# V products and their copies moved to other slots of the batch loop, in a gated cross-attention and expert block

## The reference

```python
# attention over the context, 16 heads of depth 8
q = layernorm(x) @ Wq.T + bq ; k = ctx @ Wk.T + bk ; v = ctx @ Wv.T + bv
attn = softmax(q k^T / sqrt(8))                    # per batch and head: 56 x 1500
x = x + tanh(g_xattn) * ((attn @ v) @ Wo.T + bo)
# 160 experts, the 8 with the highest sigmoid router score, and a shared expert
x = x + tanh(g_ffn) * ffn(layernorm(x))
```

## Time and profile before

| | |
|---|---|
| median of 3 runs | 1201.7 us (1195.89 to 1203.61) |
| the profiled execution | 1199.14 us, of which its span is 1197.6 us |
| granted TensorE clock, mean | 0.979 of full speed |
| instructions | 37,798 |

### The profile page before, as it was taken

One profiled execution on the slowest core, in us unless ns is written; L12 is line 12 of the kernel. 1 busy time (PEld: TensorE's weight loads), 2 busy tenths in 40 slices (PEclk: granted clock), 3 DMA queues, 4 the chain that ended last, 5 costly groups with the idle time before them and its releaser, 6 DMA issues.

```text
span 1197.6 us, 37798 instructions
## 1 busy us (share of the span) xinstructions
PE 1099.4 (92%) x12090; PEld 704.8 (59%) x12090; DVE 979.5 (82%) x1680; ACT 837.8 (70%) x1790; POOL 599.5 (50%) x1011
## 2 busy tenths in 40 slices
PE   1586989999999999999999999877999999999998
PEld 0254667767766667767766676653555555555554
DVE  2774768878788788787887888757999999999998
ACT  1343656676666676676667666656888888888887
POOL 7887588888888887888888772000000000000000
PEclk9887999999999999999999999988999999999999
DMA  8869668969878789798887863123777676777773
GB/s 134 156 124 162 140 134 174 151 149 166 145 163 154 139 169 146 152 164 145 168 151 139 168 118 74 41 90 108 225 234 234 223 240 222 236 230 229 237 224 125
DMA packets 200998, 197.04 MB, mean 165 GB/s; under 512 B 161183, under 2 KB 167391, under 8 KB 200966
## 3 DMA queue, kind: packets, MB, share of 16 engines
q1 hardware_dynamic: 189446, 175.64, 65.4%
q0 software_dynamic: 11520, 20.99, 7.0%
HBM read 109.96 MB, written 12.55 MB: 102 GB/s over the span
## 4 chain that ended last, share of the span: by engine, by line
PE 75%; DVE 7%; ACT 5%; issue 4%; DMA 4%; SPq 3%; POOL 2%; ACTq 0%; DVEq 0%; POOLq 0%
PE bank L1230 14%; PE bank L1258 14%; PE bank L1069 12%; PE bank L1083 12%; PE bank L1100 8%; PE bank L1136 5%; ACT p_exp L640 4%; PE bank L1124 4%; DMA ctT<-ctx_parts 3%; DVE rec L938 2%; DVE part_max L838 1%; SPq L378 1%; PE bank L1155 1%; DVE ctT L980 1%; PE bank L1148 1%
## 5 line engine op out<-in xcount | busy, mean ns | idle before, releaser
L640 ACT ACTIVATE p_exp<-bank 125x448 f32<-125x448 f32 x768 | 389.6, 546 | 241.9 <-PE bank L1083 241.3
L838 DVE TENSOR_REDUCE part_max<-bank 128x1 f32<-128x500 f32 x672 | 419.5, 671 | 111.5 <-PE bank L1100 110.9
L1083 PE MATMUL bank<-q_st,k_stk 97*125 97x224 f16 x1536 | 282.9, 268 | 23.7 <-ACT p_exp L640 6.9
L1100 PE MATMUL bank<-kparts,q_blk 128*128 128x500 f16 x672 | 256.3, 384 | 17.8 <-DVE part_max L838 13.2
L1083 PEld LDWEIGHTS bank<-q_st,k_stk 97*125 97x125 f16 x1536 | 184.2, 138 | 130.4 <-ACT p_exp L640 75.9
L1258 PE MATMUL bank<-ctT,w_ring 128*128 128x448 f16 x960 | 234.0, 353 | 3.0 <-DVE ctT L980 3.0
L732 ACT ACTIVATE ctT<-bank 128x448 f32<-128x448 f32 x320 | 174.0, 544 | 40.0 <-PE bank L1230 15.8
L980 DVE TENSOR_TENSOR ctT<-k_stk,ctT 128x448 f16<-128x448 f32 x320 | 198.0, 619 | 0.3 <-ACT ctT L738 0.2
L1069 PE MATMUL bank<-p_exp,v_sb 125*25 125x168 f32 (+1 forms) x6144 | 189.2, 264 | 0.6 <-ACT p_exp L640 0.6
L738 ACT ACTIVATE ctT<-k_stk 128x448 f16<-128x448 f32 x320 | 181.9, 568 | 3.5 <-DVE k_stk L974 3.5
L1230 PE MATMUL bank<-q_hi,w_ring 128*128 128x448 f16 x640 | 173.9, 353 | 2.2 <-ACT k_stk L720 2.2
(11 more groups left out here) (139 smaller groups left out, 1244.8 us busy)
## 6 DMA issues: line engine op xcount, KB each, us to landing
v_sb<-c_scratch SPq DMA_DIRECT2D x114, 448.0 KB, 3.9
k_stk<-kparts SPq DMA_DIRECT2D x384, 93.8 KB, 5.0
ctx_in<-in_ctx_dram SPq DMA_DIRECT2D x31, 750.0 KB
k_stk<-c_scratch SPq DMA_DIRECT2D x38, 448.0 KB, 4.0
w_scratch<-w_out POOLq DMA_DIRECT2D x80, 128.0 KB, 6.7
w_in<-in_L_ffn_w_gate_dram POOLq DMA_DIRECT2D x160, 32.0 KB, 4.5
w_in<-in_L_ffn_w_down_dram POOLq DMA_DIRECT2D x80, 64.0 KB, 7.7
v_sb<-c_scratch SPq DMA_DIRECT2D x6, 336.0 KB, 4.8
```

Source lines behind the costliest of these rows:

```text
L640: act.activation(p_exp[0:KP, j % PR, f * 448:(f + 1) * 448], ST[f][0:KP, 0:448], ACT.Exp).then_inc(exp_done, 1)
L838: v.reduce_max(part_max[:, i // NCH, i % NCH:i % NCH + 1], SM[i % NSM][:, 0:CK], axis=AX.X).then_inc(sm_maxed, 1)
L1083: last = pe.matmul(ST[f][0:KP, (g % 2) * GC:(g % 2 + 1) * GC], k_stk[0:97, u, g, j * KP:(j + 1) * KP], q_st[0:97, u, g, :, :].rearrange("p ...
L1100: pe.matmul(SM[i % NSM][:, 0:CK], rows, kparts[:, u, 0, c * CK:(c + 1) * CK], start=True, stop=True).then_inc(sm_done, 1)
```

## The change

The V products of a chunk move from slots 3, 7, 11 to slots 0, 4, 8. ScalarE's copies of V move from behind the second exponential of slots 4, 8 and 0 of the next step to behind the first exponential of slots 1, 5, 9; the copies now wait chunk by chunk for the value products that read the old contents. The spread product and the normalisation move from slot 5 to slot 6, the product with Wo from slot 9 to slot 11, behind the transpose of the maxima, and the update of x to the end of slot 11. The waits that guard bank 6 move with them. No instruction that computes or copies is added or removed.

```diff
-    SPREAD_AT, OUT_AT, NEG_AT = 5, 9, KT - 1
+    SPREAD_AT, OUT_AT, NEG_AT = 6, KT - 1, KT - 1
...
                         if f == 0:
                             evacuate(step, k - 1)
-                    if k == 0 and on(step, 2):
-                        values(back(step, 2), NCH - 1)
-                    elif k and k % TPC == 0 and on(step, 1):
-                        values(back(step, 1), (k - 1) // TPC)
+                        if f == 0 and k % TPC == 1 and on(step, 1):
+                            values(back(step, 1), k // TPC)
...
                 act.wait_ge(vp_done, b * NCH + (c + 1))
-                if c == 0:
-                    until(act, pv_done, (b - 1) * KT)
+                until(act, pv_done, (b - 2) * KT + (c + 1) * TPC)
...
+                evacuate(step, KT - 1)
...
-                    if on(step, 1) and k % TPC == 3:
+                    if on(step, 1) and k % TPC == 0:
                         u = back(step, 1)[1]
                         b = num(back(step, 1))
                         until(pe, v_copied, b * NCH + c)
-                        if on(step, 3) and c == 1:
+                        if on(step, 4) and c == 0 and back(step, 4)[1] == 1:
+                            pe.wait_ge(x2_done, back(step, 4)[0] + 1)
+                        if on(step, 3) and c == 2:
                             pe.wait_ge(nrm_done, num(back(step, 3)) + 1)
-                        if on(step, 3) and c == 2 and back(step, 3)[1] == 1:
-                            pe.wait_ge(x2_done, back(step, 3)[0] + 1)
...
-                            pe.wait_ge(v_copied, num(back(step, 1)) * NCH + 1)
+                            pe.wait_ge(v_copied, num(back(step, 1)) * NCH + 2)
...
+                    if on(step, 1) and k == NEG_AT:
+                        b = num(back(step, 1))
+                        pe.wait_ge(neg_made, b + 1)
+                        pe.transpose(SM[NSM - 1][0:MT, 0:64].bitcast(fp16), neg_max[:, :], ident16[:, :]).then_inc(neg_tr, 1)
                     if on(step, 3) and k == OUT_AT and back(step, 3)[1] == 1:
                         h = back(step, 3)[0]
                         if on(step, 1):
-                            pe.wait_ge(v_copied, num(back(step, 1)) * NCH + 2)
+                            pe.wait_ge(v_copied, num(back(step, 1)) * NCH + NCH)
```

More of the change, by code:

```diff
@@ L1157, in body @@
                         last.then_inc(op_done, 1)
[L1158 to L1161, removed]
                     aside(step, k, (TOKENS_REST_AT, lambda: query_tokens(2, 1, NTC)),
```

## The result

| | before | changed |
|---|---|---|
| median | 1201.93 us (4 runs) | 1171.52 us (1169.99 to 1173.53, 4 runs) |
| ratio, with its 95% interval | | 0.9757 (0.9726 to 0.9789) |
| profiled execution, its span | 1199.14, 1197.6 us | 1173.53, 1172.0 us |
| loop, us a step, from step 5 to step 31 | 21.77 | 20.90 |

A forecast was written before the change was run, and what follows sets the result against it. The prediction took TensorE, busy 92% of the span, as the bound; 20.43 + 0.40 + 0.25 = 21.08 us a step and 4.05 us at the start gave 1175.8, median 1178 us, range 1167 to 1193.

The forecast's parts named there:

- The gaps behind the exponentials: TensorE's lost time in the three light slots and the slots behind them; V products in slots 0, 4, 8 recover 1.15 us a step.
- ScalarE's copies: Copies delay the second exponential of slots 1, 5, 9; 0.25 us of margin is left, so they cost nothing.
- The new wait for VectorE: TensorE's second maximum of slot 8 waits for the maximum behind the later normalisation; 0.40 us a step.
- `o_nrm` against GpSimd: VectorE's `o_nrm` in its new slot may be delayed by GpSimd at SBUF; 0.25 us a step, between 0 and 0.76.
- GpSimd as a floor: GpSimd's own work in the loop fills 20.96 us a step; the forecast step of 21.08 lies just above it.
- my own signs of being wrong: Among them: scores in the loop wait for the row of maxima because GpSimd has fallen behind; no size given.
- Rival C: No new wait, `o_nrm` free, GpSimd's floor holds the loop at 20.96 us a step: 1175 or 1170 us; chance 0.14.
- The start: Earlier transposes and rows of q in step 3 remove TensorE's row DMA waits of 1.04 and 3.01: 4.05 us gained.
- Rival A: `o_nrm` blocked by GpSimd in nearly every step, 0.76 us each, period 21.59: about 1193 us; chance 0.16.
- Rival B: The gap only moves: V copies ahead of the second exponential delay the next slot's scores, 22.23 a step, 1211 us; chance 0.08.

The follow-up runs named there:

- e12: Changed kernel with ScalarE's copies of V behind the second exponential of slots 0, 4, 8; 1173.2 us, ratio 0.981.
- e8: Kernel before with only the spread product and normalisation moved to slot 6, V products left in slots 3, 7, 11; 1210.7 us, ratio 1.009.
- e3: Changed kernel with the spread product and normalisation back in slot 5 and GpSimd's wait for its own low parts filled; 1169.6 us, ratio 0.974.
- e2: Changed kernel with GpSimd's wait for its own low parts filled by its next piece of work; 1165.5 us, ratio 0.971.
- e5: Changed kernel run once more with no edit, on the chip of other runs; 1171.8 us, ratio 0.976.
- e4: Changed kernel with SP issuing the rows of q in steps 1 to 3 ahead of the DMA transposes; 1165.7 us, ratio 0.972.
- e9: Changed kernel with GpSimd's wait filled and the rows of q issued ahead of the transposes; 1168.7 us, ratio 0.976.
- e10: e9 with the reciprocal written back into its PSUM bank, so `o_nrm` has one input in SBUF; 1160.5 us, ratio 0.971.
- e11: Kernel before with one more 128x128 conversion on GpSimd per pair of experts; 1196.6 us, ratio 0.9995.

## Why the prediction was right, and where its terms were off

The forecast of 1178 us was 6.5 too high, within its range. 4.6 of these are the step from the profiled execution to the median: I added 2.6, as the kernel before had it, and the changed kernel's median is 2.0 below its profiled execution. The sum itself, 1175.8, was 2.3 above the 1173.53 measured. It came so close partly by luck, because errors cancelled.

- *The gaps behind the exponentials, 1.15 a step*: right. Slots 0, 4, 5 last 1.52, 1.52 and 1.81, where I had 1.51, 1.51 and 1.82, and loads' waits fell to 8.4 us (under 15 was the test).
- *ScalarE's copies, nothing*: right, by the slots of 1.82 behind them and by e12.
- *The new wait for VectorE, 0.40*: right, 0.40 between starts. The reciprocal indeed started 0.58 behind the spread product. I had expected 18 us or so of these waits in all; the profile counts 8.3, since it leaves out the latency and `o_nrm` added little. e8 is no second proof of the term: its 0.39 is a net of two effects, and it is the V products that wait there, not a maximum. And I costed the term by the place of one instruction. e3 shows that it belongs to VectorE's pace from slot 3 on and does not go when the instruction moves.
- *`o_nrm` against GpSimd, 0.25*: wrong in size. Its mean is some 0.06 above 0.39 in the loop of the changed kernel, where it had been 0.23 above in the kernel before. I had bounded it by the earlier trace rows and picked a third. What the runs showed in its place is that it depends on the distance between GpSimd and TensorE, and that distance is fixed as soon as one waits for the other: the cost was near 0 where GpSimd was late (changed kernel), and 0.18 in nearly every step where it was early (e2).
- *GpSimd as a floor at 20.96*: right as a number (20.90 measured), but I treated it as a bound that would not be touched. It was: four steps of the loop (22.28, 21.89, 22.65 and 23.34 where 21.07 is usual) hold 5.9 us more, 0.23 a step. Three of them hold a wait for the row DMA, one an `o_nrm` of 1.2 us. Scores that wait for this row in the loop were one of my own signs of being wrong, and it showed. That is nearly what I had put down for `o_nrm`, so the sum held for the wrong reason. Rival C's mechanism took part in the result.
- *Missed*: slot 11. Without the V products, its transpose starts 0.78 behind the value products (420.25 against 419.47), where the V products had started 0.90 behind them, and the next scores follow after 0.15. So the slot is 1.53 us long rather than 1.80, and in every second step, the one without the product with Wo, slot 0 behind it gives 0.17 back (1.69 where 1.52 is usual). Undisturbed steps came out at 20.27 and 21.07, a mean of 20.67 where my terms give 20.83.
- *The start, 4.05 us*: half wrong. The wait of 1.04 at 130.81 went, the 3.01 did not. Two steps of my reasoning failed. The first is the date of the rows of q. SP was indeed no longer held by V products (5.2 us of waits within the 13.05 us below, none within the 9.35), but the first transpose was issued 1.84 us later than before and the three took 1.5 us longer by themselves, so the rows came 1.9 us earlier, not 4 to 5, and `q_blk` waited 10.85 where I had 8. SP in the kernel before:

```profile
113.19 13.05 SPq L334 DMA_TRANSPOSE ctT<-ctx_parts  x3
126.34 2.44 SPq L326 DMA_DIRECT2D q_stk<-q_hi  x4
```

  The second is that I moved the rows and left TensorE where it was. Its wait began 1.9 us earlier as well (154.13 - 3.03 = 151.10 against 153.00), so nothing of it went. e5 shows that this matters more than the date. SP's rows and TensorE's wait in e5:

```profile
121.09 2.44 SPq L326 DMA_DIRECT2D q_stk<-q_hi  x4
...
150.73 0.40 PE L1081 MATMUL bank<-q_st,k_stk 97*125 97x224 f16 x2 [3.01 <-DMA q_st<-neg_row]
```

  The rows came 5.3 us earlier than in the kernel before, more than I had expected, TensorE was there 5.3 us earlier too, and the wait was still 3.01. It went only where the rows stand ahead of the transposes (e4, e9, e10) or GpSimd's wait is filled (e2, e3). Why TensorE's date and that of the rows move together was not tested. The start was 3.0 us shorter in the profiled executions, and e5, 3.4 us shorter again with the same code, shows that this is within what its DMAs vary.

Rival A (`o_nrm` blocked in every step) did not come; e2 and e3 show that it is real and what would have brought it. Rival B is ruled out by e12 and by the slots.

## What to carry to other kernels

Measure the slots of a hand-scheduled loop by the distance between starts, and fill the slots in which another engine's latency, not work, sets the length: here 2.07 us of V products moved into three such slots took 1.15 us of gaps a step without removing an instruction. Before counting the gain, work out how much time each other engine has in hand over the loop, and when something that an engine waits for is moved, ask whether the engine itself arrives earlier as well; with GpSimd 0.8 us a step from its limit, the last of the gain was already its. Once two engines run in a fixed relation, a conflict between them stops being random: it comes in nearly every step or in nearly none.

## What the runs showed of the hardware

- A VectorE product of 128x224 float32 with both inputs in SBUF took 391 ns at least and up to 1996 ns beside GpSimd (e2; 391 to 392 in 21 of 26 loop steps of the changed kernel); with one input in PSUM it took 391 to 392 ns in all 32 executions (e10).
- More work on GpSimd can leave a kernel no slower and its loop shorter: e11's loop took 21.62 us a step against 21.77, in the profiled executions, and `o_nrm` then took 0.7 us at most instead of 1.39 (its mean fell by 0.16, the period by 0.15).
- SP spent 9.35 us on the issue of three DMA transposes in step 3 with no wait for another engine among them, while other DMAs were in flight; whatever is queued behind them starts that much later.
